# A routed expert layer whose slots run with the second product one slot late, in ascending order of expert size, with both weight buffers in use to the end

## What is computed

```python
for d in range(depth):                       # depth 4, 16 leaves
    logits = xf @ Wr[off:off + cnt].T + br[off:off + cnt]
    sel = jnp.take_along_axis(logits, leaf[:, None], axis=1)[:, 0]
    leaf = leaf * 2 + (sel > 0).astype(jnp.int32)
onehot = jax.nn.one_hot(leaf, E_, dtype=xf.dtype)

def body(acc, params):
    w1, bb1, w2, bb2, m = params
    h = jax.nn.gelu(xf @ w1 + bb1, approximate=False)
    y = h @ w2 + bb2
    return (acc + m[:, None] * y, None)
```

## Time and profile before

| | before |
|---|---|
| median of 3 runs | 1835.92 us (1829.23 to 1841.54) |
| profiled execution, first to last instruction | 1832.5 us |
| TensorE busy, mean granted clock | 1658.9 us (91%), 0.942 |
| VectorE, ScalarE, GpSimd busy | 850.0, 472.2, 128.8 us |
| HBM traffic | 228 MB read, 129 GB/s over the span |
| the slots | from 1277.6 us to 1575.2 us of the span |

### The profile page before, as it was taken

One profiled execution on the slowest core, in us unless ns is written; L12 is line 12 of the kernel. 1 busy time (PEld: TensorE's weight loads), 2 busy tenths in 40 slices (PEclk: granted clock), 3 DMA queues, 4 the chain that ended last, 5 costly groups with the idle time before them and its releaser, 6 DMA issues. The chain is left out here.

```text
span 1832.5 us, 26087 instructions
## 1 busy us (share of the span) xinstructions
PE 1658.9 (91%) x8767; PEld 1029.9 (56%) x8768; DVE 850.0 (46%) x2173; ACT 472.2 (26%) x928; POOL 128.8 (7%) x193
## 2 busy tenths in 40 slices
PE   6889889999999999898999999998899988799964
PEld 3345564476457589896576766656334433464532
DVE  6665376821266674523733426534233322513464
ACT  2012224430020132221636116411223321231220
POOL 0011000000000003431100000001000000200000
PEclk9798999999999899898999989998999989899996
DMA  5131126200071078863000102045998784230000
GB/s 157 63 117 34 43 84 235 80 12 0 10 295 35 25 283 261 272 185 90 4 23 24 72 32 80 1 184 193 427 429 359 300 372 189 83 105 1 0 1 28
DMA packets 69900, 237.69 MB, mean 130 GB/s; under 512 B 14232, under 2 KB 17935, under 8 KB 62913
## 3 DMA queue, kind: packets, MB, share of 16 engines
q1 hardware_dynamic: 54155, 207.34, 30.2%
q0 software_dynamic: 15664, 29.30, 5.4%
HBM read 228.18 MB, written 8.39 MB: 129 GB/s over the span
## 5 line engine op out<-in xcount | busy, mean ns | idle before, releaser
L101 PE MATMUL psum<-ahead_arena 125*125 125x257 f32 (+2 forms) x720 | 218.3, 461 | 4.5 <-DVE ahead_W L2449 3.4
L101 PEld LDWEIGHTS psum<-ahead_arena 125*125 125x125 f32 (+1 forms) x720 | 131.1, 189 | 82.0 <-issue 66.1
L715 DVE TENSOR_SCALAR a0e_ring<-a0e_node,a0e_key 125x625 f16 x198 | 70.2, 388 | 69.8 <-PE psum L520 64.2
L101 PE MATMUL psum<-a_W,1_xn_turned 128*125 128x512 f32 x200 | 91.0, 605 | 1.2 <-DVE a_u L1346 1.2
L518 PE MATMUL psum<-a0e_ring,a0e_tables 125*128 x198 | 74.1, 434 | 18.2 <-DVE a0e_ring L715 10.9
L101 PE MATMUL psum<-a_W,a0l_H 128*125 128x512 f32 x190 | 81.9, 592 | 0.7 <-issue 0.7
L2836 PE MATMUL psum<-ahead_arena,ahead_W 128*32 128x256 f32 x928 | 77.4, 396 | 5.7 <-DMA ahead_arena<-in_L_ffn_W 5.7
L101 PE MATMUL psum<-e_xgT,e_W 128*128 128x156 f32 x512 | 73.0, 306 | 3.0 <-issue 3.0
L101 PEld LDWEIGHTS psum<-e_xgT,e_W 128*128 128x128 f32 x512 | 71.6, 198 | 3.8 <-issue 3.7
L2863 PE MATMUL psum<-ahead_arena,ahead_W 128*32 128x512 f32 x464 | 65.6, 595 | 7.6 <-DMA ahead_arena<-in_L_ffn_W 7.6
L3144 DVE TENSOR_TENSOR ahead_W<-psum,ahead_W 128x256 f32<-128x256 f32 x58 | 24.6, 424 | 97.6 <-PE psum L2849 70.3
(11 more groups left out here) (692 smaller groups left out, 2919.7 us busy)
## 6 DMA issues: line engine op xcount, KB each, us to landing
ahead_arena<-in_L_ffn_W SPq DMA_DIRECT2D x52, 2048.0 KB, 12.6
e_W<-in_L_ffn_W SPq DMA_DIRECT2D x16, 2048.0 KB, 11.0
1_xn_turned<-half_shares SPq DMA_DIRECT2D x16, 256.0 KB, 8.8
a_stage<-in_L_gnn_W SPq DMA_DIRECT2D x8, 512.0 KB, 7.5
ahead_arena<-in_L_gnn_W SPq DMA_DIRECT2D x2, 2048.0 KB, 10.4
a_W<-in_L_gnn_W SPq DMA_DIRECT2D x3, 1024.0 KB, 5.4
a_qkv<-half_shares SPq DMA_DIRECT2D x11, 256.0 KB, 3.3
a_W<-in_L_ffn_w_down POOLq DMA_DIRECT2D x1, 2816.0 KB, 16.2
```

The source lines that it names most:

```text
L101: last = nc.tensor.matmul(bank[0:rows, at:at + cols], lhs, rhs, start=(n == 0), stop=(n == len(terms) - 1))
L715: nc.vector.tensor_scalar(ring[:, bass.ds(at, 1), 0:NODES].rearrange("p a n -> p (a n)"), node[:, :], key[:, k, bass.ds(t, 1)], None, ALU. ...
```

## The change

Nothing outside `layer2_ffn` changes except the layout of two weight arrays and the size of two buffers.

- **First product.** `hid` is one bank; 16 matmuls of 512 columns (`w1`, L2854) take the place of 32 of 256. The two `wa` pieces are now split by contraction (rows 0 to 255 of `W1`, rows 256 to 511) and no longer by hidden half, so the second piece is awaited in the middle of `w1`.
- **Second product one slot late.** On TensorE slot s is `w1(s)`, then `w2_before(s)`, the second product of slot s-1 (L2874), then `turn_hidden(s)`, all four transposes together (L2862).
- **ScalarE** copies 512 columns once, copies the sums of slot s-1, applies GELU once to 512 columns.
- **VectorE** does `gather(s)`, `add_bias(s)` (one add of 512 columns, L3208), `fold_before(s)` (three adds, L3216, L3219, L3223) in this order.
- **Slot 0** runs inside the sort: its first product after the fifth of the eight sort products, its transposes after the sixth, its second product after the seventh.
- **Order.** Others run in ascending number of rows after expert 0 (2, 3, 3, 4, 4, 6, 16, 53, 73, 91, 97 rows), so eight experts of one slot alternate with eight heavy slots, then one heavy slot, then slots of 2, 3, 3 and 4. For these last the two buffer sets alternate, since the heavy expert is done.
- **Tables.** `tab_i` has 6 x 64 words and lists slots; VectorE makes it with more small operations and two rounds through TensorE. In VectorE's loop over pairs of slots there is one table load per two slots (`slot_at`, L2719), in the loop over the last 12 slots one per slot.
- **Bias rows.** The gather of `b2` and the five adds to `c.x` move from before the slots to behind the heavy slots (L3264); the heavy expert's loads no longer wait for them.

```diff
-        Wa = [[ahead.piece("a", b, a).rearrange("p (c g n) -> p c g n", c=CH, g=QT) for a in range(2)] for b in range(2)]
+        Wa = [[ahead.piece("a", b, a).rearrange("p (c g n) -> p c g n", c=CH // 2, g=QT) for a in range(2)] for b in range(2)]
...
+                    def w1(b, s, loaded):
                         pe.wait_ge(wa_landed[b][0], loaded)
                         pe.wait_ge(sem["tokens_ready"], s + 1)
                         for k in range(CH):
+                            if k == CH // 2:
+
+                                pe.wait_ge(wa_landed[b][1], loaded)
                             for g in range(QT):
                                 last = nc.tensor.matmul(
-                                    hid[0][g * SL:(g + 1) * SL, 0:HC], xgT[:, k, :], Wa[b][0][:, k, g, :],
+                                    hid[g * SL:(g + 1) * SL, :], xgT[:, k, :], Wa[b][k // 2][:, k % 2, g, :],
                                     start=(k == 0), stop=(k == CH - 1))
...
+                    with pe.Fori(1, pairs) as n:
+                        loaded = visit_of(pe, n) * 16 + 16
+                        w1(OTHERS, 2 * n, loaded)
+                        w2_before(HEAVY, 2 * n, 16)
+                        turn_hidden(2 * n)
+                        w1(HEAVY, 2 * n + 1, 16)
+                        w2_before(OTHERS, 2 * n + 1, loaded)
+                        turn_hidden(2 * n + 1)
...
+                    def gather(s, place):
+                        dve.wait_ge(sem["hidden"], s + 1)
+                        nc.vector.tensor_copy(xgT[:, :, :], xsT[:, :, bass.ds(place, SL)]).then_inc(
                             sem["tokens_ready"], 1)
...
+                    def slot(s, place, e):
+                        gather(s, place)
+                        add_bias(s, e)
+                        fold_before(s)
...
+                    with dve.Fori(1, pairs) as n:
+                        place, e = slot_at(dve, n)
+                        slot(2 * n, place, e)
+                        slot(2 * n + 1, heavy_place(n), heavy_e)
```

More of the change, by code:

```diff
@@ new lines, in _ @@
+                    for v, of in enumerate([eid[:, 0:1], ends[:, 4:5], ends[:, 6:7]]):
+                        nc.tensor.matmul(small[0:1, 132 + RUNS * v:132 + RUNS * (v + 1)], of, of_visit, start=True,
+                                         stop=True)
+                    for v, (of, by) in enumerate([(c.ones[0:EXP2, 0:1], places), (eid[:, 0:1], inside),
+                                                  (before[:, 0:1], inside)]):
+                        last = nc.tensor.matmul(small[0:1, 288 + LIST * v:288 + LIST * (v + 1)], of, by, start=True,
+                                                stop=True)
@@ L3047, in _ @@
                                                 ALU.is_equal).then_inc(sem["moves_made"], 1)
+                    end, heavies, pairs, rem, start, longer, count, rest = [col(ends, n) for n in range(8)]
+                    visit, slot0, token0 = [col(before, n) for n in range(3)]
+                    light_slots = col(V, 2)
                     dve.wait_ge(sem["spread"], 1)
-                    nc.vector.tensor_copy(tot[:, :], small[0:1, 260:266])
-                    nc.vector.tensor_copy(before[:, :], small[0:EXP2, 256:259]).then_inc(done.sem, 1)
@@ new lines, in _ @@
+                    listed_slots, runs_left, run0, half, couples, beyond_v, listed_all, total = [
+                        col(one, n) for n in range(8)]
+                    number, tot_light = tot[0:1, 0:1], tot[0:1, 1:2]
+                    heavies, pairs = heavies[0:1, :], pairs[0:1, :]
+                    numbers = row[0:1, 0:RUNS]
+                    nc.vector.tensor_tensor(listed_slots, tot_light, col(tot2, 1), ALU.add)
+                    nc.vector.tensor_scalar(run0, number, -1.0, col(tot2, 0), ALU.add, ALU.min)
@@ new lines, in _, with heavy_place @@
+                    nc.vector.tensor_copy(own[:, :], ownf[:, :]).then_inc(sem["tail_known"], 1)
+                    add_bias(0, 0)
+                    pairs, heavies, all_listed = pairs_of(dve), heavies_of(dve), listed(dve)
+                    base, heavy_e, slots = heavy_start(dve), heavy_expert(dve), slots_of(dve)
+                    def heavy_place(n):
+                        return within(base + n * SL, 0, NOWHERE)
+                    dve.wait_ge(sem["sorted_freed"], 2 * CH)
+                    slot(1, base, heavy_e)
@@ L3166, in _ @@
+                    dve.wait_ge(sem["rows_added"], TILES)
+                    with dve.Fori(pairs, all_listed) as n:
+                        place, e = slot_at(dve, n)
+                        slot(heavies + n, place, e)
+                    dve.wait_ge(sem["y_ready"], slots)
                     dve.sem_inc(sem["y_ready"], 1)
```

646 lines of the change are left out of this document (343 added, 303 removed).

## The result

| | before | after |
|---|---|---|
| median of 4 runs each | 1833.99 us (1829.23 to 1841.54) | 1907.29 us (1903.13 to 1911.97) |
| profiled execution, first to last instruction | 1832.5 us | 1906.4 us |
| TensorE busy, mean granted clock | 1658.9 us, 0.942 | 1650.0 us, 0.923 |
| the sums of the last slot are copied | 1575.16 us | 1651.51 us |

The changed kernel is slower: the ratio is 1.0407, with a 95% interval of 1.0368 to 1.0445. The span grew by 73.9 us, and the end of the slots moved by 76.3 us, so the difference arises in the slots; 2.4 us come back in the rest of the program.

A forecast was written before the change was run, and what follows sets the result against it. Two close limits bound the kernel: transfers, 19.6 us an expert, and TensorE, 18.2 us for two slots. Span 1832.5 plus 45 (slots) plus 62 (clock) gives 1939.5, with 3.4 for the median 1943 us; range 1875 to 1985.

The forecast's parts named there:

- The mechanism: In every slot TensorE's next first product waits for VectorE's gather, behind bias add and fold: 3.4 or 4.2 us idle.
- The marks of the wait: Signs: idle of 3.4 to 4.2 us before L2854 some 28 times, no waits for `ahead_arena`, DMA share near 0.6.
- The marks of the clock: Signs over the slots: granted clock near 0.8, slots of 13 to 15 us, stage ending about 1680 us.
- chain term: Slots with their gaps, without the clock: the stage ends at 1620 us against 1575.2 before, 45 us later.
- Work of a slot: TensorE's two products, four transposes and drain: 3.44 + 3.44 + 0.8 + 0.2 = 7.9 us.
- The table load: A table load on VectorE between fold and gather lengthens the gap by 0.8 us, from 3.4 to 4.2 us.
- The end: After the last slot, bias add, GELU and last second product with nothing beside them: 5.1 us.
- The clock: TensorE's clock falls after each of 26 gaps, costing 2.4 us a gap, 62 us; bounds nothing and 104 us.
- Every gap pays?: Claim that each of the 26 TensorE gaps costs clock time, as the skill's rule has it; 2.4 us each.
- The clock holds: Rival: TensorE stays at 2.4 GHz through gaps of 3.4 us, only 45 us remain, 1881 us; chance 0.13.
- The clock hardly recovers: Rival: TensorE's clock costs 4 us a gap, 104 us in all, 1985 us; chance 0.12.
- The slots do overlap: Rival: TensorE finds the next gather done, gaps some 0.3 us, 36 us earlier, 1800 us; chance 0.04.

The follow-up runs named there:

- the filled gap: Changed kernel with four matmuls of no use to the result behind each slot's transposes, in place of most of each gap: 1872.17 us, ratio 1.0223.
- the last kernel: Gather-first kernel plus two y buffers, bias-row fetches ahead of the last four stores, their adds ahead of the last bias add: 1789.34 us, ratio 0.9755.
- the first version of it: Changed kernel with VectorE gathering slot s+1 before the bias add and fold of slot s: 1810.28 us, ratio 0.9868; run again, 1807.53 us.
- the two orders with an early gather: Changed kernel with VectorE's next gather ahead of bias add and fold (1810.28 us), or between bias add and fold (1820.89 us).

## Why the prediction was right, and where it was off

**The mechanism** was as predicted: the gather behind the fold makes TensorE wait in every slot. The marks of the wait are there: 27 gaps ahead of L2854, 26 of 3.1 to 4.0 us and one of 7.3 with the bias-row adds, no waits for `ahead_arena`, a DMA share of 0.62. The marks of the clock are there in part: 0.85 over the slots, where I had named "near 0.8", and slots of 10.7 to 15.0 us, where I had 13 to 15; 9 of 26 are shorter than that. The stage ended at 1651, where I had it near 1680.

**The sum** gave 45 + 62 = 107 us for what measured 76.3 us. Without the clock the stage would have ended at some 1606 us and not at 1620:

| term | predicted | measured |
|---|---|---|
| slot 1 begins | 1286 | 1284.5 |
| slot 1 with its gap | 9.3 | 8.7 |
| slots 2 to 28, work | 27 x 7.9 = 213 | 27 x 7.66 = 206.8 |
| 26 gaps behind slots 2 to 27 | 107 | 99.4 |
| end | 5.1 | 6.9 |
| clock | 62 | 45.2 |

The measured terms come to 1284.5 + 8.7 + 206.8 + 99.4 + 6.9 = 1606.3, and 45.2 more to 1651.5. Without the clock the stage would so end 31 us later than the 1575.2 before; that is the true chain term, where I had 45.

- *Work of a slot.* The 0.2 us that I allowed for draining the array is at most 0.1: the transposes come 3.54 us behind the start of the second product, where the first product takes 3.46, and four take 0.66 us, not 0.8.
- *The table load.* I had taken 0.8 us for a load in the chain. The gap is 3.28 us inside a pair and 3.77 between pairs, so 0.5; in the last twelve slots it is 3.95, 0.67 more. The load took 305 ns (307 in the earlier trace rows). By the floor that the Trainium skill gives in "DMA: Bandwidth & Descriptors", section "Latency and other measured facts", the step would have been larger than mine; the trace went the other way.
- *The end.* I had not seen that the last second product also waits for the fold (`w2_before` waits on `y_ready`): 3.2 us where I had 1.6.
- **The clock is the term that was mis-sized**: 2.4 us a gap predicted, 1.6 measured (42.4 us over 27 first products, and 2.8 in the last second product). I had two rows to choose from, 3.2 us lost behind two gaps at 1494 and 1.4 us behind the one of 3.90 us at 1536, took the middle, rounded it up, and argued it with "the next gap follows". The gap of 3.90 us was the row nearest in length, and its 1.4 us was nearly right: 26 x 1.4 = 36 us would have given 1832.5 + 45 + 36 + 3.4 = 1917 us. That it came so near is in part luck, since single ones of these gaps cost from nothing to 2.9 us. The pair at 1494 was two gaps, and its 3.2 us was the price of two.
- *Every gap pays?* No. Six of the 27 first products behind a gap run in 3.46 us, the others in 5.15 to 6.4. The section "HAM oscillation — how this bites in real kernels" of "TensorE: Matmul & The Clock Gate" in the Trainium skill, which has every tile start cold, describes the direction rightly and is too strong for this case.

**The rivals.** "The clock holds" is excluded by the filled gap: about 38 us come back when TensorE doesn't stand still. "The clock hardly recovers" (4 us a gap) is excluded by 1.6 us, and even gaps of 5.2 to 6.1 us (one of 9.5) cost 2.1. "The slots do overlap" became an experiment. With the gather first they do: my 1800 us for it stands beside the 1797 us that were measured once the store was out of the way (1789 us in the last kernel), and the 19.6 us for a pair that I gave as the transfers' bound stands beside 20.0 us, from the first product at 1355.31 to that of the next pair at 1375.31, in the first version of it. What I had missed there is that a store would then count.

## What to carry to other kernels

When two engines hand work to each other once per step, write down for each hand-over what stands ahead of it in program order on the engine that serves it. An operation whose input is ready early and whose output is awaited first belongs ahead of everything that waits for something late; here exchanging two blocks was worth 97 us. A software pipeline that removes one cover also shortens the step under which other slow things lay (a store, a fetch), so look at the slowest of each and not at the median, and keep small indirect fetches away from stretches in which large transfers fill the DMA engines. For a cost that the trace bounds from two sides, take the row nearest in kind, not the middle, and keep the range wide, since one row is one sample.

## What the runs showed that I had not expected

- Five indirect fetches of 125 rows of 2 KB (1.28 MB in all) took 11.3 to 24.5 us to land at the start of the slots and 17.4 to 42.7 us in the middle of them, and 3.9 to 5.5 us with no weights under way. A 64 KB store behind them took 20.3 to 22.0 us in the two orders with an early gather, 31.7 and 41.6 us with the fetch moved to the middle, and no more than 9.7 us in the changed kernel, where the median is 5.5. Why the changed kernel was spared is not shown. While they last, the DMA engines stay fully busy at 350 to 370 GB/s in place of 430, and a 2048 KB weight piece takes 27.6 us (18.5 in that part without them). The Trainium skill, "DMA: Bandwidth & Descriptors", section "Queues, rings and completion order", says that a DMA engine takes turns between its queue rows packet by packet. That would make a queue of small pieces slow beside one of large pieces; the runs agree with it and don't isolate it.
- Gaps of TensorE of 1.1 us, 27 of them, cost no clock; gaps of 3.1 to 4.0 us (one of 7.3) cost 1.6 us each on the mean, and gaps of 5.2 to 6.1 us (one of 9.5) 2.1 us each, in a stream that else was dense.
- With equal gaps of 3.95 us the price alternates (5.15, 5.86 us for the same 32 matmuls in turn). In the pairs, with gaps of 3.77 and 3.28 us in turn, it was 1.7 us and mostly nothing. So one gap of a trace is a poor sample for 27.
